# The Relu's output to the tokens' partitions: VectorE's turned blocks and DMAs in place of TensorE's transposes

## The reference

```python
xn = _layernorm(x, axis=-1)
# attention: a two-layer MLP before a sliding window of 65 keys
h = relu(xn @ nm_w1 + nm_b1)
m = h @ nm_w2 + nm_b2
q, k, v = m @ q_w + q_b, m @ k_w + k_b, m @ v_w + v_b
weights = softmax(where(valid, q . k_band / sqrt(128), -inf))
attn = weights . v_band
# experts: each token uses 8 of 16
scores = sigmoid(xn @ gate_w.T)
_, inds = top_k(scores + expert_bias, 8)
combine = one_hot(inds) * 2.826 * selected / sum(selected)
h = silu(hg) * hu
y = sum over the experts of (h @ w_down) * combine
y = y + silu(xn @ sg.T) * (xn @ su.T) @ sd.T
out = x + attn + y
```

## Time and profile before

| | |
|---|---|
| three plain runs | 696.60, 696.91, 698.62 us (median 696.91) |
| profiled execution | 698.64 us, span 696.90 us, granted clock 0.995 in the mean |
| TensorE busy | 685.6 us, 98% of the span |
| VectorE busy | 582.7 us, 84% |
| ScalarE busy | 437.7 us, 64% |
| GpSimd busy | 443.0 us, 64% |
| DMA | 93.94 MB, queue q1 46.9% of 16 engines |
| chain that ended last | PE 92%, DVE 4%, ACT 2% |

### The profile page before, as it was taken

The page is one execution under the profiler, slowest core; times in us unless marked ns, Lnnn a source line. Parts: engine busy times, 40 slices in busy tenths (PEclk is TensorE's granted clock), DMA queues, the critical chain, the costliest instruction groups (busy, mean ns, idle before and its releaser), DMA issues.

```text
span 696.9 us, 10439 instructions
## 1 busy us (share of the span) xinstructions
PE 685.6 (98%) x3232; PEld 562.1 (81%) x3232; DVE 582.7 (84%) x1625; ACT 437.7 (63%) x874; POOL 443.0 (64%) x400
## 2 busy tenths in 40 slices
PE   8989999999999999999999999999999999999997
PEld 6768788888888888888888888888888888888886
DVE  6988888978889787888978889787888978788775
ACT  4766665766666566765766566566665666566573
POOL 4684567567666666667567666666667567665553
PEclk8999999999999999999999999999999999999999
DMA  8816327182652728337192562727337171641800
GB/s 263 195 36 177 129 85 250 33 236 67 141 194 65 227 69 187 125 93 242 34 225 77 135 199 64 227 75 184 121 105 231 35 239 48 140 165 34 225 1 16
DMA packets 84536, 93.94 MB, mean 135 GB/s; under 512 B 8320, under 2 KB 74624, under 8 KB 84480
## 3 DMA queue, kind: packets, MB, share of 16 engines
q1 hardware_dynamic: 84480, 93.28, 46.9%
HBM read 88.49 MB, written 4.77 MB: 134 GB/s over the span
## 4 chain that ended last, share of the span: by engine, by line
PE 92%; DVE 4%; ACT 2%; issue 1%; DMA 1%; SPq 0%; DVEq 0%
PE ps_u L442 26%; PE ps_y L452 26%; PE ps_g L432 26%; PE bank L374 3%; PE bank L413 3%; PE bank L396 3%; PE ps_y L422 2%; PE bank L403 1%; PE bank L379 1%; DVE ps_u L1069 1%; PE bank L385 1%; DMA exp_raw<-wexp 1%; DVE h_lo L1075 1%; ACT h_hi L682 0%; ACT prob L663 0%
## 5 line engine op out<-in xcount | busy, mean ns | idle before, releaser
L1194 POOL TENSOR_TENSOR silu_c<-silu,comb_b 128x512 f32<-128x512 f32 x252 | 325.4, 1294 | 229.4 <-ACT silu L674 227.5
L682 ACT ACTIVATE h_hi<-ps_u 128x512 fp32r<-128x512 f32 x272 | 162.6, 598 | 242.7 <-DVE ps_u L1069 242.3
L1075 DVE TENSOR_TENSOR h_lo<-ps_u,h_hi 128x512 fp32r<-128x512 f32 x272 | 185.8, 683 | 47.8 <-ACT h_hi L682 44.2
L1069 DVE TENSOR_TENSOR ps_u<-silu_c,ps_u 128x512 f32<-128x512 f32 x256 | 176.4, 689 | 30.5 <-PE ps_u L442 26.0
L674 ACT ACTIVATE silu<-ps_g 128x512 f32<-128x512 f32 x272 | 162.1, 596 | 1.1 <-PE ps_g L432 1.0
L442 PE MATMUL ps_u<-xn_hi,exp_w_hi 128*128 128x512 f32 x272 | 111.1, 408 | 2.7 <-DVE h_lo L1075 2.6
L452 PE MATMUL ps_y<-h_hi,exp_w_hi 128*128 128x512 f32 x272 | 110.2, 405 | 0.4 <-DVE h_lo L1075 0.4
L432 PE MATMUL ps_g<-xn_hi,exp_w_hi 128*128 128x512 f32 x272 | 108.3, 398 | 0.1
L452 PE MATMUL ps_y<-h_lo,exp_w_hi 128*128 128x512 f32 x272 | 107.4, 395 | 0.0
L442 PE MATMUL ps_u<-xn_hi,exp_w_lo 128*128 128x512 f32 x272 | 107.4, 395 | 0.0
L452 PE MATMUL ps_y<-h_hi,exp_w_lo 128*128 128x512 f32 x272 | 107.3, 394 | 0.0
(11 more groups left out here) (152 smaller groups left out, 988.6 us busy)
## 6 DMA issues: line engine op xcount, KB each, us to landing
comb_b<-c_dram SPq DMA_DIRECT2D x63, 1024.0 KB, 12.1
mom_b<-st_dram SPq DMA_DIRECT2D x13, 512.0 KB, 3.7
xres<-x_t SPq DMA_DIRECT2D x16, 256.0 KB, 2.6
out_t<-xres SPq DMA_DIRECT2D x16, 256.0 KB, 2.2
xin<-x SPq DMA_DIRECT2D x15, 256.0 KB, 3.0
xn<-x_t SPq DMA_DIRECT2D x13, 256.0 KB, 3.5
exp_raw<-wexp SPq DMA_DIRECT2D x3, 768.0 KB, 10.5
exp_raw<-wexp SPq DMA_DIRECT2D x2, 384.0 KB, 6.8
```

The source lines that it names most:

```text
L682: A(h_t[hbuf(par, s)][0][:], ps_u[(par + s) % 2][:], ACT.Copy).then_inc(s_h_hi, 1)
L1069: V.tensor_tensor(ps_u[i][:], src[:], ps_u[i][:], ALU.mult).then_inc(s_h, 1)
L1075: V.tensor_tensor(t[1][:], ps_u[(par + s) % 2][:], t[0][:].bitcast(F32), ALU.subtract)\
L1194: G.tensor_tensor(silu_c[i][:].rearrange("p (l x) -> p l x", l=RUNS), silu[i][:].rearrange("p (l x) -> p l x", l=RUNS), comb_b[:, :, s1 - ...
```

## The change

From group 1 on, TensorE no longer turns hid. In its place:

- VectorE turns hid in blocks of 32x32 within each group of 32 partitions (hid_blocks, one instruction over 128x512, step 12 of the group before), into a part of exp_raw.
- SyncE stores the result in DRAM in four pieces of 64 KB (store_hid), so that the blocks of the same tokens come together, and loads it back as 256 KB (load_hid) into another part of exp_raw, hid_m. The load stands between the first and the second spread of the weights. All of it comes at step 12 instead of 13.
- ScalarE's high part is read from hid_m, in step 9 in place of 0, and VectorE's rest in step 10 in place of 1. The key sums stay in steps 1 and 2 and are read from hid_m too, so both of their inputs, and both of hid_n_lo's, lie in SBUF.
- The Relu (hid_relu) moves from step 13 to 11. The statistics of a later group move from step 12 to 15, their variance from 13 to 0 of the next group.
- In group 0, ScalarE makes the high parts of the value weights and of the query-key product before the weights of experts 1 and 2, and expw_hi(9) and (10) come before q_hi. The query projection of TensorE moves behind the up projection of step 3. The turn of hid stays on TensorE there.

```diff
+        spare = exp_raw[:].rearrange("p s c -> p (s c)")
+        hid_b = spare[:, 3 * T:4 * T].rearrange("p (q c) -> p q c", q=4)
+        hid_m = spare[:, 4 * T:5 * T].rearrange("p (q c) -> p q c", q=4)
...
+        moved = hid_m.rearrange("p q (a f) -> p a q f", f=32)
+
+        def quarters(t):
+            return t.rearrange("p a (q f) -> p a q f", q=4)
...
+            def store_hid(g):
+                sp.wait_ge(S["hid_b"], g)
+                for t in range(4):
+                    sp.dma_start(h_dram[t * 32:(t + 1) * 32, :, :].rearrange("t q c -> q t c"), hid_b[:, t, :])\
+                        .then_inc(s_hid_st, 16)
+
+            def load_hid(g):
+                sp.wait_ge(s_hid_st, 64 * g)
+                if g > 1:
+                    sp.wait_ge(S["hn_lo"], g)
+                    sp.wait_ge(S["key_term"], 2 * g)
+                sp.dma_start(hid_m, h_dram).then_inc(s_hid_m, 16)
...
-                if s == 13 and not last(g):
+                if s == 12 and not last(g):
                     store_comb(g + 1, 1 - par)
-                    for c in range(NCHUNK):
+                    store_hid(g + 1)
+                    spread(g + 1, 1 - par, 0, False)
+                    load_hid(g + 1)
+                    for c in range(1, NCHUNK):
                         spread(g + 1, 1 - par, c, False)
...
                     fresh_weights(3, bank[2])
-                    hid_turn(0)
+                    hid_turn()
                     pe.wait_ge(s_scw, 1)
                     pe.wait_ge(s_row, 1)
-                    pe.wait_ge(s_fresh, 3)
-                    q_proj(0)
...
-                if s == 16 and more:
-                    hid_turn(g + 1)
...
                 up_proj(g, par, s)
+                if first(g) and s == 3:
+                    pe.wait_ge(s_fresh, 3)
+                    q_proj(0)
...
+                    act.wait_ge(S["pv"], g)
+                    act.wait_ge(s_hid_m, 16 * g)
+                    A(quarters(hid_n[0][:]), moved, ACT.Copy).then_inc(S["hn_hi"], 1)
...
-                elif s == 0:
+                elif s == 9:
                     hid_n_hi(g)
...
-                if s == 13 and more:
+                if s == 11 and more:
                     hid_relu(g + 1)
...
+            def hid_blocks(g):
+                dve.wait_ge(S["hid"], g + 1)
+                if g == 1:
+                    dve.wait_ge(s_expw, STEPS)
+                else:
+                    dve.wait_ge(s_hid_st, 64 * (g - 1))
+                V.transpose(hid_b.rearrange("p q c -> p (q c)"),
+                            hid[:].rearrange("p (a q t) -> p q a t", a=TILES, q=4)).then_inc(S["hid_b"], 1)
...
+                    V.tensor_tensor(quarters(hid_n[1][:]), moved, quarters(hid_n[0][:]).bitcast(F32),
+                                    ALU.subtract).then_inc(S["hn_lo"], 1)
...
-                if s == when(g, 1, 4):
+                if s == when(g, 10, 4):
                     hid_n_lo(g)
...
+                if s == 0 and TURNED < g + 2 < GROUPS:
+                    variance(g + 2)
+                if s == 12 and more:
+                    hid_blocks(g + 1)
+                if s == 13 and first(g):
+                    moments(g + 2, par)
+                if s == 15 and TURNED < g + 3 < GROUPS:
                     moments(g + 3, 1 - par)
```

More of the change, by code:

```diff
@@ L70, in hdist, with layer @@
     return next(d for d in range(1, 2 * STEPS + 1) if order[(p - d) % (2 * STEPS)] == order[p])
-def layer(nc, x, x_t, watt, watt_t, expert_bias, wexp, out_t, c_dram, st_dram):
+def layer(nc, x, x_t, watt, watt_t, expert_bias, wexp, out_t, c_dram, st_dram, h_dram):
     ctx = ExitStack()
@@ L214, in layer @@
         names = """bn aggr var_eps rstd mean centred0 centred1 xn xn_tp xn_hi xn_lo gate_mm gate_h gate_s gate_e
-            gate_1 score select top8 rest weight wsum winv comb comb_t
+            hid_b gate_1 score select top8 rest weight wsum winv comb comb_t
             hid_mm hid hid_hi hid_lo q_mm q_hi q_lo hid_tp hn_hi hn_lo key_term
@@ L219, in layer @@
         S = {n: sem(n) for n in names}
+        s_hid_st = sem("hid_stored")
+        s_hid_m = sem("hid_loaded")
         s_comb_st = [sem(f"comb_stored{i}") for i in range(2)]
@@ L296, in store_comb, with spread @@
                 sp.dma_start(c_dram[par], comb_t[:]).then_inc(s_comb_st[par], 16)
+            def spread(g, par, c, fresh):
                 sp.wait_ge(s_comb_st[par], 8 * (g + (2 - par)))
-            def spread(g, par, c, fresh):
                 if not fresh and g + c > 1:
@@ L464, in q_proj, with hid_turn @@
                 project(bank[1], 1, hid_t).then_inc(S["q_mm"], 1)
-            def hid_turn(g):
-                pe.wait_ge(S["hid_lo"], g + 1)
+            def hid_turn():
+                pe.wait_ge(S["hid_lo"], 1)
                 turn(bank[0], hid).then_inc(S["hid_tp"], 1)
@@ L567, in att_early @@
                     pe.wait_ge(S["xn_lo"], g + 2)
-                    pe.wait_ge(S["hn_lo"], g + 1)
-                    pe.wait_ge(S["key_term"], 2 * g + 2)
+                    pe.wait_ge(S["hid_hi"], g + 1)
+                    if first(g):
+                        pe.wait_ge(S["hn_lo"], 1)
+                        pe.wait_ge(S["key_term"], 2)
                     gate(1 - par)
@@ L651, in hid_n_hi @@
             def hid_n_hi(g):
-                act.wait_ge(S["hid_tp"], g + 1)
-                A(flat(hid_n[0]), bank[0][:], ACT.Copy).then_inc(S["hn_hi"], 1)
+                if first(g):
+                    act.wait_ge(S["hid_tp"], 1)
+                    A(flat(hid_n[0]), bank[0][:], ACT.Copy).then_inc(S["hn_hi"], 1)
+                else:
+                    act.wait_ge(S["pv"], g)
+                    act.wait_ge(s_hid_m, 16 * g)
+                    A(quarters(hid_n[0][:]), moved, ACT.Copy).then_inc(S["hn_hi"], 1)
             def z_hi(g):
@@ L689, in prologue @@
                 xn_hi(0, 0)
-                expw_hi(1)
-                expw_hi(2)
                 act.wait_ge(s_merge, 1)
@@ L695, in prologue @@
                 A(chain[:, 0, :], ps_y[:, M_A:M_A + P], ACT.Copy, scale=SCALE).then_inc(s_qk, 1)
+                expw_hi(1)
+                expw_hi(2)
                 gate_exp(0)
@@ L716, in fresh_att @@
                 if s == 3:
-                    q_hi(0)
                     hid_n_hi(0)
@@ L720, in fresh_att @@
                     expw_hi(10)
+                    q_hi(0)
                 if s == 4:
@@ L888, in q_lo @@
                     .then_inc(S["q_lo"], 1)
+            def hid_blocks(g):
+                dve.wait_ge(S["hid"], g + 1)
+                if g == 1:
+                    dve.wait_ge(s_expw, STEPS)
+                else:
+                    dve.wait_ge(s_hid_st, 64 * (g - 1))
+                V.transpose(hid_b.rearrange("p q c -> p (q c)"),
+                            hid[:].rearrange("p (a q t) -> p q a t", a=TILES, q=4)).then_inc(S["hid_b"], 1)
             def hid_n_lo(g):
                 dve.wait_ge(S["hn_hi"], g + 1)
-                V.tensor_tensor(flat(hid_n[1]), bank[0][:], flat(hid_n[0]).bitcast(F32), ALU.subtract)\
-                    .then_inc(S["hn_lo"], 1)
+                if first(g):
+                    V.tensor_tensor(flat(hid_n[1]), bank[0][:], flat(hid_n[0]).bitcast(F32), ALU.subtract)\
+                        .then_inc(S["hn_lo"], 1)
+                else:
+                    V.tensor_tensor(quarters(hid_n[1][:]), moved, quarters(hid_n[0][:]).bitcast(F32),
+                                    ALU.subtract).then_inc(S["hn_lo"], 1)
             def key_terms(g, seq):
@@ L899, in key_terms @@
                     dve.wait_ge(s_vec2, 1)
+                if not first(g):
+                    dve.wait_ge(s_hid_m, 16 * g)
                 for a in range(2 * seq, 2 * seq + 2):
+                    tile = bank[0][:, a * P:(a + 1) * P].rearrange("p (q f) -> p q f", q=4) if first(g) \
+                        else moved[:, a, :, :]
                     done = V.tensor_tensor_reduce(
-                        out=key_prod[:, a, :], in0=bank[0][:, a * P:(a + 1) * P], in1=key_row[:], scale=1.0,
+                        out=quarters(key_prod[:])[:, a, :, :], in0=tile,
+                        in1=key_row[:].rearrange("p (q f) -> p q f", q=4), scale=1.0,
                         scalar=vecs[:, 6:7], op0=ALU.mult, op1=ALU.add, accum_out=key_term[:, a:a + 1])
@@ L1023, in att @@
                         variance(g + 2)
-                if s == 12 and TURNED < g + 3 < GROUPS:
-                    moments(g + 3, 1 - par)
[L1026 to L1030, removed]
+                if s == 0 and TURNED < g + 2 < GROUPS:
[5 more added lines that the diff above has]
+                if s == 15 and TURNED < g + 3 < GROUPS:
+                    moments(g + 3, 1 - par)
                 if s == 14:
@@ L1246 @@
     st_dram = nc.dram_tensor("st_dram", (2, T), F32, kind="Internal").ap()
-    layer(nc, *args, out_t, c_dram, st_dram)
+    h_dram = nc.dram_tensor("h_dram", (P, 4, P), F32, kind="Internal").ap()
```

(1 more changed line is left out.)

## The result

The changed kernel takes 701.26 us in the median of six runs (700.87 to 702.94), the kernel before 696.81 (six runs, 696.20 to 698.63). The ratio is 1.0056, 95% interval 1.0043 to 1.0069: slower by 0.6%. The forecast was 698.0 in a range of 690 to 706, with most weight on no change (0.42), then slower (0.37). The time lies in the range; the likeliest sign was missed.

The account below looks back on a forecast made before the run. TensorE was taken to bound the groups from 1 on. Transposes -6.6, stalls +9.2 and first group -1.5 gave +1.1, so 699.7 us for an execution like the profiled one, less 1.73: 698.0 us, range 690 to 706.

Parts of the forecast that it names:

- The transposes: TensorE's four transposes of hid at step 16 go: 0.44 us saved, 15 times, 6.6 us in all.
- The stall at step 10: hid_n_lo on VectorE makes h_lo late for TensorE's step 11 up projection: 0.66 us in groups 1 to 14, 9.2 us.
- Group 15: No routing in these steps, so VectorE has room for hid_n_lo; no stall counted there.
- The edits priced at nothing: Turned blocks, statistics, key sums, ScalarE's moved passes and the transfer queue fall in free time or cover: price 0.
- the first group: ScalarE's new order and the moved query projection in group 0 gain net 1.5 us, bounds 0.5 and 3.5.
- the shift to the median: Profiled run had TensorE's clock at half early; median assumed without that, so 1.73 us is taken off the sum.
- both terms whole and part of the slow clock gone: Upper bound of the first group's gain: 3.5 us.
- The weight pass loses the port: Rival: step 10's weight pass waits behind GpSimd's product, 1.17 us more per group, 16.4 in all, 714.4 us; chance 0.11.
- VectorE absorbs the pass: Rival: VectorE hides hid_n_lo at step 10, stall term between 0 and 5.6 us, time 688.8 to 694.4; chance 0.22.
- The load is late: Rival: the load of the blocks lands late, key sums wait 5.5 us, 70 us in all, 768; chance 0.04.
- The first group gives nothing: Rival: group 0 gains nothing because its chain is bound elsewhere, 699.5 us; chance 0.06.

Follow-up runs that it names:

- third experiment: Changed kernel with hid_n_lo still in step 10 but behind p_lo instead of ahead of it: 697.32 us, ratio 0.9993 to the kernel before.
- The second: Changed kernel with hid_n_hi on ScalarE at step 1 and hid_n_lo on VectorE at step 2, behind the key sums: 694.85 us.
- the fifth: Changed kernel with hid_n_lo on VectorE in step 12, behind the turned blocks: 690.89 us, ratio 0.9902 to the kernel before.
- experiment 1: Kernel before with only the group 0 changes (ScalarE's order, query projection behind step 3's up projection): 696.82 us, ratio 0.9983.
- 4: Changed kernel with group 0 put back as in the kernel before: 701.64 us, ratio 1.0048 to the kernel before.
- 8: Changed kernel with hid_n_lo in step 12, group 0 as in the kernel before, plus four idle matmuls at its start: 691.12 us.
- experiment 7: Kernel before with four idle TensorE matmuls where it waits for the bias vectors, nothing else: 697.12 us, ratio 0.9989.
- the sixth: Changed kernel with a second, unread turn of hid in blocks ahead of the first in step 12: 701.91 us, ratio 1.0069 to the kernel before.

## Why the prediction was right and where it was wrong

**The transposes: right.** -0.44 was forecast, -0.43 measured, 15 times.

**The stall at step 10: right in place and mechanism, a tenth short in size.** Forecast 0.66 in 14 groups, measured 0.73. The lag of h_lo was 0.89 against 0.86, the hand-over to TensorE 0.06 against 0.03, the restart of TensorE 0.10 against 0.08. That is 1.0 us in all. The third experiment shows 0.28 of each 0.73 to be the port and 0.45 the pass; the forecast had 0.26 and 0.40. The second and the fifth show that nothing else of the change causes it: with the pass elsewhere the stall is gone whole.

**Group 15: missed.** "Group 15 has no routing in these steps and so room": it lost 0.19. It had room for the pass, but not for a port wait of 0.5 (1.16 in place of 0.67); behind p_lo, without that wait, nothing is lost.

**The edits priced at nothing: right.** The blocks were 0.70 long (0.8 taken), and doubled still cost the groups from 1 on nothing. The load landed at 192.6, as forecast (issue, time to landing), and the key sums asked for it at 193.57:

```profile
184.84 0.33 SPq L315 DMA_DIRECT2D exp_raw<-h_dram  x1
```

```profile
exp_raw<-h_dram SPq DMA_DIRECT2D x1, 256.0 KB, 7.8
```

```profile
193.57 0.38 DVE L960 CUSTOM_DVE_ANT_0 key_prod<-exp_raw,key_row,vecs 128x128 f32<-128x128 f32 x1
```

The forecast had them ask at 194.8; the cover was 1 us and not 2, and in group 8, where the load took 8.5 us, 0.3. The Relu two steps earlier put hid_lo under a product of GpSimd, 1.11 us in the mean in place of 0.69 (1.17 in 14 groups), and that did not reach TensorE:

```profile
L922 DVE TENSOR_TENSOR hid_lo<-hid,hid_hi 128x512 fp32r<-128x512 f32 x16 | 17.8, 1112 | 0.0
```

**The step that failed: the first group and the shift to the median.** The forecast counted -1.5 for the first group in an execution like the profiled one, "both terms whole and part of the slow clock gone" being only its far end, and then took off another 1.73 because plain runs have no slow clock. The profiled difference is -1.49, but that the number fits is luck: its mechanism gave nothing. The new order gains nothing at full clock (experiments 1, 4 and 8) and at most 0.1 us at half clock (the profiles of experiment 1 and the kernel before). The forecast took 0.7 back for the waits for h_lo; they grew by 1.4, and the lead of 2.67 at step 3 was all lost. And a lead of that size comes without the order: the profile of experiment 7, with the old order and a shorter stretch at half clock (3.4 us in place of 6.8, added up from the granted clock of each microsecond), is 1.42 ahead of the profile before at step 14 of group 0 and 1.49 at the end. So it is the clock, not the order. There was nothing left to subtract for the median, and the two terms took the same gain twice. With the shift left out, the forecast's own sum is 699.7, and with the 1.0 of the stalls and the 0.2 of group 15 added 700.9, against 701.26. I had also taken the median run of the kernel before to be one without the slow clock; of the 40 later runs, 6 were. Why the clock stays up in one execution and falls in the next stays open: with the wait for the vectors gone it fell less often (1 of 12 runs at 0.995 or below, 18 of 40 before), not never.

The net of the forecast, +1.1 us, is a quarter of the measured +4.4, and the time lies in the range because that range was 16 us wide.

**The rivals.** *The weight pass loses the port*: the tie came as drawn, both recorded at 175.61, and VectorE won it: 0.21 in all 14 groups, and the product 1.35 in place of 1.29. In group 0 of the same execution, and of experiments 2, 3, 5 and 6, the pass is recorded 0.03 or 0.04 behind the product and lost, 1.32 to 1.34 in place of 0.21:

```profile
48.77 1.28 POOL L1255 TENSOR_TENSOR silu_c<-silu,comb_b 128x512 f32<-128x512 f32 x1 [1.67 <-ACT silu L715]
48.80 1.32 DVE L897 SCALAR_TENSOR_TENSOR weight<-rest,score 128x64 f32<-128x64 f32 x1
```

So the two outcomes lie a few hundredths of a microsecond apart, 16 us hung on them, and this part of the forecast was right by as little. *VectorE absorbs the pass*: false in step 10, true in step 12. *The load is late*: not in the changed kernel's profile; once in the fifth experiment's, where the period is shorter, by 0.82, and three times in the sixth's, by 0.2 to 0.4. *The first group gives nothing*: true at full clock and nearly so at half, and given 0.06 where it deserved most of the weight, since its gain was read off an execution in which the clock was at half.

## What to carry to other kernels

Work taken off the bounding engine pays only if the passes that replace it go where the helper engine has room against every reader behind it: list for each step the cover to every wait of the bounding engine, not only to the usual one (step 10 had 0.31 us against h_lo, step 2 had 0.43 against the output pass, step 12 had 0.8), and mind what the neighbour engine runs at that moment. The same pass gave 701.3 and 697.3 us in step 10 (ahead of p_lo and behind it), 694.9 in step 2 (with ScalarE's hid_n_hi at step 1) and 690.9 in step 12, by its place. Where the helper engine sets the pace, as in group 0 here, work taken off the other's path gains nothing. And before a gain is taken from the start of a kernel, look whether the profiled execution had TensorE's clock at full there; a saving measured across a clock step is not a saving of the schedule.

## What the runs showed of the hardware

- VectorE turns 128x512 in blocks of 32x32 in 0.70 us in one instruction, where 32 partitions by 128 elements, read from a PSUM bank, take 0.311: four times the length, four times the partitions, little more than twice the time.
- A subtraction with both inputs in SBUF (0.674 in the third experiment) takes as long as one with an input in PSUM (0.676, hid_n_lo of group 0). The Trainium skill's page VectorE: DVE Perf Modes (The TRN2 errata) has the SBUF form 62 cycles shorter; no run here shows that.
- Two instructions that exclude each other and are recorded to start within 0.04 us can go either way: VectorE first at 0.00 (175.61 both), last at 0.03 (48.80 behind 48.77).
- The 40 later runs of the kernel before spread over 3.5 us (696.05 to 699.51) in the order of their mean granted clock (1.000 down to 0.995); in its profile, the stretch at half clock lies between 10 and 18 us. Other kernels here have runs at 1.000 that are 1.3 to 1.8 us above their median, so the clock is not the only thing that spreads runs.
